# Moving the rounding and clipping to int8 from VectorE to ScalarE and GpSimd in the last phase

## The reference, cut to what matters

```
x = x + attention(layernorm(x)) @ Wo + bo      # 16 heads of 16, causal, softmax
h = layernorm(x)
scale_row = max(|h|, over the 256 columns, at least 1e-12) / 127
q = clip(round(h / scale_row), -127, 127)      # int8
x = x + (q @ q_weight) * scale_row * weight_scale
```

## Time and profile before

| | |
|---|---|
| median of 3 runs | 2089.18 us (2076.88 to 2106.33) |
| profiled execution | 2088.25 us |
| its span, first to last instruction | 2086.5 us |
| last phase | from 1891.5 to the end, 195.0 us |
| busy in the span | PE 83%, DVE 77%, ACT 61%, POOL 13% |
| busy in the last phase | PE 126.9 us, DVE 140.6 us, ACT 80.3 us, POOL 79.4 us |

### The profile page before, as it was taken

One profiled execution on the slowest core, in us unless ns is written; L12 is line 12 of the kernel. 1 busy time (PEld: TensorE's weight loads), 2 busy tenths in 40 slices (PEclk: granted clock), 3 DMA queues, 4 the chain that ended last, 5 costly groups with the idle time before them and its releaser, 6 DMA issues. The chain is left out here.

```text
span 2086.5 us, 33292 instructions
## 1 busy us (share of the span) xinstructions
PE 1741.6 (83%) x12735; PEld 595.2 (29%) x12735; DVE 1596.8 (77%) x2161; ACT 1267.8 (61%) x1587; POOL 263.6 (13%) x315
## 2 busy tenths in 40 slices
PE   5969767888888888888988888888888888887764
PEld 3646312222222222222222222222222222224442
DVE  5525597888888888888788978887888888504776
ACT  2323103767777777677677767776777677794443
POOL 4000000001110101010100000110101010113443
PEclk9989755999999999999899989998999899998876
DMA  2444100010110101010101010100001010042662
GB/s 83 144 152 128 55 0 11 14 40 27 28 27 28 40 28 39 15 41 14 40 14 40 14 40 25 30 27 27 27 28 38 22 34 20 24 125 72 189 185 90
DMA packets 102448, 105.72 MB, mean 51 GB/s; under 512 B 19092, under 2 KB 85912, under 8 KB 102296
## 3 DMA queue, kind: packets, MB, share of 16 engines
q1 hardware_dynamic: 102296, 103.60, 16.8%
HBM read 60.56 MB, written 42.47 MB: 49 GB/s over the span
## 5 line engine op out<-in xcount | busy, mean ns | idle before, releaser
L748 ACT ACTIVATE prob<-psum 128x1024 f32<-128x1024 f32 (+3 forms) x1280 | 1091.0, 895 | 529.2 <-PE psum L644 523.8
L858 DVE TENSOR_REDUCE pmax<-psum 128x2 f32<-128x1024 f32 (+2 forms) x1264 | 1154.8, 962 | 183.9 <-PE psum L596 110.8
L660 PE MATMUL psum<-prob,V 128*32 128x512 f32 (+3 forms) x5120 | 629.6, 565 | 3.5 <-ACT ust L738 3.3
L644 PE MATMUL psum<-Q,K 50*128 50x512 f16 (+3 forms) x2560 | 580.4, 360 | 12.1 <-ACT prob L748 11.2
L596 PE MATMUL psum<-K,Q 48*128 48x512 f16 x1536 | 397.8, 408 | 156.0 <-DVE pmax L858 146.8
L765 POOL TENSOR_SCALAR_AFFINE_SELECT prob<-prob 128x512 f32<-128x512 f32 x256 | 163.1, 637 | 1699.4 <-ACT prob L748 1699.4
L596 PEld LDWEIGHTS psum<-K,Q 48*128 48x128 f16 x1536 | 97.1, 94 | 656.0 <-DVE pmax L858 492.4
L644 PEld LDWEIGHTS psum<-Q,K 50*128 50x128 f16 x2560 | 157.9, 95 | 103.6 <-ACT prob L748 71.4
L615 PE MATMUL psum<-K,Q 48*128 48x512 f16 (+3 forms) x1024 | 187.0, 323 | 0.0
L610 PE MATMUL psum<-mask,maskid 64*128 64x128 bf16 (+2 forms) x1280 | 147.0, 244 | 46.1 <-DVE pmax L858 34.2
L858 DVE TENSOR_REDUCE pblk<-psum 128x8 f32<-128x1024 f32 (+1 forms) x192 | 159.0, 863 | 28.1 <-PE psum L615 24.3
(11 more groups left out here) (104 smaller groups left out, 720.3 us busy)
## 6 DMA issues: line engine op xcount, KB each, us to landing
unnormalised<-ust SPq DMA_DIRECT2D x64, 256.0 KB, 2.5
xs<-in_L_attn_x SPq DMA_DIRECT2D x16, 512.0 KB, 5.3
q_parts<-part SPq DMA_DIRECT2D x64, 128.0 KB
k_parts<-part SPq DMA_DIRECT2D x64, 128.0 KB
Q<-q_parts SPq DMA_DIRECT2D x128, 64.0 KB, 2.3
K<-k_parts SPq DMA_DIRECT2D x128, 64.0 KB, 2.1
f_us<-unnormalised SPq DMA_DIRECT2D x32, 256.0 KB
f_rs<-inverse_sums SPq DMA_DIRECT2D x32, 256.0 KB
```

The lines of the kernel that those rows point to most:

```text
L644: m = nc.tensor.matmul(PS[:, SB + 2 * pair + half, 0:CH - lo], K[it % 2][rows, pair, kb * P:(kb + 1) * P], Q[it % 2][rows, pair, c * CH + ...
L660: m = nc.tensor.matmul(PS[32 * h:32 * h + 32, UB, lo:CH], V[:, it // NG * NT + kb, col:col + 32], prob[(it * NSTEP + k) % PRING][:, h, 0:C ...
L748: nc.scalar.activation(prob[g % PRING][:, 2 * pair:2 * pair + 2, 0:n], PS[:, SB + 2 * pair:SB + 2 * pair + 2, 0:n], ACT.Exp, scale=by).the ...
L858: nc.vector.tensor_reduce(to, of, axis=AX.X, op=ALU.max).then_inc(mx_free, 1)
```

## The change

The `hq` buffers and the semaphore `hq_ready` go. A constant column `magic` of 128x1 is set once by POOL. ACT's `over_scale` computes Identity(hn * inv + MAGIC), with `magic` as the per-row bias, and writes `hr` directly. `integers` leaves DVE's list and stands in POOL's, between `divide(n+4)` and `residual(n)`; there it is two tensor_scalar passes of 128x1024, one with max and min, one that subtracts MAGIC and writes bf16, with a wait on the semaphore `clipped` between them.

```diff
-        hq = [sb(f"hq{s}", [P, TPC, D]) for s in range(2)]
+        magic = sb("magic", [P, 1])
...
+            def integers(b, c):
+                n, s = b * NCH + c, c % 2
+                pool.wait_ge(rounded, n + 1)
+                nc.gpsimd.tensor_scalar(hr[s][:], hr[s][:], MAGIC - 127.0, MAGIC + 127.0, ALU.max, ALU.min
+                                        ).then_inc(clipped, 1)
+                pool.wait_ge(clipped, n + 1)
+                if n >= 2:
+                    pool.wait_ge(hT_ps, n - 1)
+                nc.gpsimd.tensor_scalar(hi[s][:], hr[s][:], MAGIC, None, ALU.subtract).then_inc(hi_ready, 1)
...
+            nc.gpsimd.memset(magic[:], MAGIC).then_inc(magic_set, 1)
 
             def step(b, c):
                 ahead(b, c, 4, divide)
+                ahead(b, c, 1, integers)
                 ahead(b, c, 0, residual)
...
                 act.wait_ge(inv_ready, n + 1)
+                if n == 0:
+                    act.wait_ge(magic_set, 1)
+                if n >= 2:
+                    act.wait_ge(hi_ready, n - 1)
                 for t in range(TPC):
-                    i = nc.scalar.activation(hq[c % 2][:, t, :], hn[c % 2][:, t, :], ACT.Copy,
-                                             scale=inv[s][:, t:t + 1])
-                i.then_inc(hq_ready, 1)
+                    i = nc.scalar.activation(hr[c % 2][:, t, :], hn[c % 2][:, t, :], ACT.Identity,
+                                             scale=inv[s][:, t:t + 1], bias=magic[:, 0:1])
+                i.then_inc(rounded, 1)
...
-            def integers(b, c):
-
-                n, s = b * NCH + c, c % 2
-                dve.wait_ge(hq_ready, n + 1)
-                nc.vector.tensor_scalar(hr[s][:], hq[s][:], MAGIC, MAGIC - 127.0, ALU.add, ALU.max
-                                        ).then_inc(rounded, 1)
-                dve.wait_ge(rounded, n + 1)
-                nc.vector.tensor_scalar(hi[s][:], hr[s][:], MAGIC + 127.0, MAGIC, ALU.min, ALU.subtract
-                                        ).then_inc(hi_ready, 1)
...
                 ahead(b, c, 2, minus_mean_over_std)
-                ahead(b, c, 1, integers)
             steps(dve, step)
```

More of the change, by code:

```diff
@@ L915, in finish @@
         inv_ready = sem("inv_ready")
-        hq_ready = sem("hq_ready")
+        magic_set = sem("magic_set")
         rounded = sem("rounded")
+        clipped = sem("clipped")
         hi_ready = sem("hi_ready")
```

## The result

Four runs of the changed kernel gave 2141.08 to 2152.32 us, median 2148.26, against 2090.78 of the kernel before (four runs): ratio 1.0265, 95% interval 1.0214 to 1.0315. The forecast was 2098 us, within 2% of before, in a range up to 2121; the result lies above it. The profiled execution took 2144.78 us, its span is 2143.1.

What follows compares the result with a forecast made beforehand. In the last phase no engine is full; a circle of load, divide and projection sets the steps. Steps +14.4, start +1.3, end -6.3 give +9.4 us on 2088.25, 2097.6; the median stands 0.9 higher: 2098 us, range 2079 to 2121.

Steps and rivals of the forecast that it cites:

- the price of POOL's passes: Two new passes on POOL in each chunk: 1.1 us each, 2.3 for both with a gap, range 2.0 to 4.9.
- The rival for over 2%: POOL itself becomes the price: over 2% slower from 3.05 us a pass, 2140 us at 3.5; chance 0.06.
- 9 I - 12.5: Net change in us for large I, the time of both POOL passes: six pairs, the start, and twice at the end.
- The steps: Twelve steps from chunk 3 to 15: a pair takes 24.5 us, six pairs 147.0 against 132.6, +14.4 us.
- Start: Start of the last phase: POOL ends the first integers at 1913.7, where transposes began at 1912.44, +1.3 us.
- End: From the last projection to the end, where DVE's list was the bound: 26.7 us instead of 33.0, -6.3 us.
- the 8.0 that was taken: PE's time in us from the transposes to the end of the projection in a loading step, running through.
- The place in the queue: POOL's integers(n+1) stands behind divide(n+4), which waits for its DMAs, so the circle now holds integers and transpose too.
- ACT's bias: The bias column in ACT's scaling in the last phase: +0.4 us a chunk, hidden.
- The circle of the loads: Last phase: load, divide and projection wait for each other, 20.6 us for two steps; two such circles are interleaved.
- The 1.5 us a pair above the bare circle: Chunks 3 to 15 before the change: 22.1 us a pair; in some steps hi, delayed by POOL, releases PE.

Runs made afterwards that it cites:

- m_passes: The kernel before with sixteen extra POOL passes at its very start, when no other engine computes; 2128.38 us, one run.
- a_cheap: The changed kernel with both POOL passes written as multiply by 1 and add, clip not computed; 2099.12 us, ratio 1.0033 to the kernel before.
- a_reorder: The changed kernel with integers(n+1) ahead of divide(n+4) in POOL's list; 2116.56 us, ratio 1.0132 to the kernel before.
- a_early_load: The changed kernel with each load waiting for y_ready at n - 1 instead of n + 1; 2112.29 us, ratio 1.0086 to the kernel before.
- b_act_rounds: The kernel before with ACT rounding by the bias and DVE making the integers in one pass, without the lower clip; 2089.18 us, ratio 0.9947.
- b_early_load: The kernel before with each load waiting for y_ready at n - 1 instead of n + 1; 2087.38 us, ratio 0.9980.
- b_hi_first: The kernel before with DVE's integers(n+1) moved from behind scaled(n, 1) to behind scaled(n, 0); 2087.29 us, ratio 0.9937.
- b_early_hi_first: The kernel before with both the earlier loads and DVE's integers behind scaled(n, 0); 2069.39 us, ratio 0.9887.

## Why the prediction was wrong

**The step that failed is the price of POOL's passes.** The prediction put it as "the new passes have one input, so I take 1.1 us each", between 0.98 and 2.44 us. They took 3.63 and 2.78 us, 6.4 for both instead of 2.3, each above the upper end. The bounds came from a memset, a select and a tensor_tensor, rows of other operations; none of them was an end for this one. m_passes shows that the price belongs to the operation itself, and a_cheap that it was the step that mattered: with passes of 1.04 us in the same place the kernel is 0.3% slower than before, where the prediction had 0.4%. The rival for over 2% named this mechanism and its threshold, 3.05 us a pass; the mean of the two is 3.2. It got 0.06 for a reason that was none: that no 128x1024 pass of another kind had taken longer.

**With the measured price the other terms hold in part.** By 9 I - 12.5 and I = 6.4 the net is +45; measured are +53.5 in the last phase. The steps: 22.2 + 6.4 is 28.6 a pair, six are 171.6, measured 175.7. Start 5.4, measured 6.4. End: by the terms +0.7, measured +4.0. From the transposes to the end of the projection PE took 7.2 to 9.1 us, 8.2 in the mean, so the 8.0 that was taken holds. The 8 us that the terms leave unexplained are not traced.

**The place in the queue** was right: `integers` ran right behind `divide`, all transposes were released by POOL, and a_reorder and a_early_load take back 26 and 32 of the 53.5 us at the same price. What the sum left out is POOL's own list: at the measured price it is 11.1 us a step, and in 5 of the 12 loading steps POOL was still at it when the load had landed.

**The end** was credited with -6.3 us. In a_cheap it gives -3.8; the rest of the difference is not traced. b_act_rounds got 5.7 us at this place without the passes on POOL.

**ACT's bias** cost what was said: the row below stands against 27.0 us for L1065, 0.4 us a chunk. It is hidden in the steps: from 1930 to 2106 us POOL waited for it once, for 2.1 us.

```profile
L1082 ACT ACTIVATE f_hr<-f_hn,f_magic,f_inv 128x256 f32<-128x256 f32 x64 | 33.0, 588 | 0.0
```

**The circle of the loads, "with no slack anywhere",** was right and not the whole: b_early_load shows a second bound right behind it. The 1.5 us a pair above the bare circle, 9 us in twelve steps, was read as the cost of the holds. b_hi_first doesn't answer this, since `divide` held the pass instead. In b_act_rounds the pass is nearly free (mean 790 ns), and its steps are shorter by 3.5 of those 9 us. What the rest is stays open; that m_passes, with more holds, has longer steps speaks for the holds, and is no proof.

The Trainium skill, page "GPSIMD Engine Reference", section "Elementwise — side-by-side cycle accounting", gave 1.03 cycles per element for a light body. The trace agrees for multiply and add: 1.05 us for 1024 elements, which is 0.88 us at that rate and 0.17 around it. It does not for max, min and subtract: 3.63 and 2.77 us are 4.3 and 3.2 cycles of 1.2 GHz per element.

## What to carry to other kernels

Before work moves to POOL, look for a row of that very operation with those very operators on POOL, or measure it alone; the rows of other passes of the same size bound nothing. A step put behind an instruction that waits for a transfer enters the circle of the transfers with its full price, even where it is cheap. Where removing a wait brings nothing, look at which row has grown in its stead: here the hold of DVE was next, and the earlier loads paid only once it was gone. And a phase that took 194.9 us in one execution took 209.5 in another with the same instructions: read a small gain from many runs, and from a trace only what a row shows.

## What the runs showed of the hardware

- A tensor_scalar on POOL, 128x1024 f32, took 3.63 us with max and min or min and subtract, 2.77 with max or subtract alone, and 1.05 with multiply and add; a cast to bf16 took 1.04. Subtracting MAGIC took 1.04 us written as multiply by 1 and add its negative (a_cheap), and 2.78 as a subtraction. The output's type, f32 or bf16, made no difference to the subtraction alone (2.77 both).
- The price of max and min was the same beside busy engines as alone (3630 and 3632 ns).
- A pass of DVE over SBUF alone, 0.69 us, waits for the whole of POOL's instruction: mean 2465 ns where `residual` starts ahead of it in 14 of 16 chunks (b_early_load), 694 where nothing of POOL does (b_early_hi_first). The tiny `row_scales` is held as well (1.78 us in a_reorder).
